# Perceiver kernel on one core: the first head pair's key rows by selection matmuls, early keys and values among the maxima

## The reference

```
q = einsum(layernorm(x), wq) * 8 ** -0.5          # 16 heads of 8
k = einsum(ctx, wk);  v = einsum(ctx, wv)         # 2048 keys per batch
logits = einsum(k, q) + mask                      # the mask is all zeros in these inputs
x = x + einsum(softmax(logits), v) @ wo
```

## Time and profile before

| | |
|---|---|
| runs | 303.33 us median of 3 (302.24 to 303.79) |
| profiled execution | span 302.6 us from first to last instruction; no other time is given for it |
| instructions | 10,326 |
| PE, DVE, ACT, POOL busy | 94%, 75%, 69%, 23% of the span |
| DMA | 28.06 MB, 93 GB/s on average |

### The profile page before, as it was taken

One profiled execution on the slowest core, in us unless ns is written; L12 is line 12 of the kernel. 1 busy time (PEld: TensorE's weight loads), 2 busy tenths in 40 slices (PEclk: granted clock), 3 DMA queues, 4 the chain that ended last, 5 costly groups with the idle time before them and its releaser, 6 DMA issues.

```text
span 302.6 us, 10326 instructions
## 1 busy us (share of the span) xinstructions
PE 284.7 (94%) x4336; PEld 186.6 (62%) x4340; DVE 226.9 (75%) x376; ACT 207.3 (69%) x447; POOL 71.0 (23%) x140
## 2 busy tenths in 40 slices
PE   7965999999999999899999899999999999999995
PEld 6553666666767675453656567676766665436675
DVE  5864789999999985464478998988999970744583
ACT  4638489889898888723445898989989987233350
POOL 6595500020011102431021865000011020110001
PEclk9995899999999999999999999999999999999999
DMA  7984513632222280233200036422221200000000
GB/s 238 410 248 138 169 41 106 232 119 71 87 70 80 80 301 6 104 122 105 89 3 0 3 84 213 136 79 74 79 82 54 57 2 2 0 3 2 0 0 20
DMA packets 10898, 28.06 MB, mean 93 GB/s; under 512 B 2241, under 2 KB 3329, under 8 KB 10466
## 3 DMA queue, kind: packets, MB, share of 16 engines
q1 hardware_dynamic: 10776, 27.16, 27.3%
q10 hardware_dynamic: 74, 0.20, 0.2%
HBM read 20.74 MB, written 6.62 MB: 90 GB/s over the span
## 4 chain that ended last, share of the span: by engine, by line
PE 75%; DVE 14%; DMA 3%; ACT 3%; POOL 2%; issue 2%; ACTq 1%; DVEq 0%; POOLq 0%
PE bank L1082 73%; DVE mx L835 7%; DMA k_first_rows<-kparts 2%; ACT probs L557 1%; DMA kpair<-k_first_rows 1%; DVE kparts L804 1%; DVE k_rest L801 1%; DVE s_neg L894 1%; DVE st L745 1%; POOL m_rows L438 1%; PE bank L1387 1%; ACTq L276 1%; PE bank L1427 0%; DVE xn L764 0%; DVE negm L842 0%
## 5 line engine op out<-in xcount | busy, mean ns | idle before, releaser
L835 DVE TENSOR_REDUCE mx<-bank 128x2 f32<-128x1024 f32 x128 | 153.0, 1222 | 19.1 <-PE bank L1082 15.2
L557 ACT ACTIVATE probs<-bank 128x512 f32<-128x512 f32 x256 | 139.3, 595 | 20.7 <-PE bank L1082 16.7
L1082 PE MATMUL bank<-q_exp,kpair 64*128 64x128 bf16 x1024 | 84.8, 218 | 1.9 <-ACT probs L557 1.2
L1082 PE MATMUL bank<-probs,v_all 128*9 128x128 f32 x2048 | 80.1, 274 | 1.1 <-ACT probs L557 1.0
L1082 PE MATMUL bank<-kpair,q_rows 64*128 64x512 bf16 x256 | 73.9, 388 | 5.8 <-DMA kpair<-k_first_rows 5.8
L1082 PEld LDWEIGHTS bank<-q_exp,kpair 64*128 64x128 bf16 x1024 | 55.3, 94 | 31.5 <-ACT probs L557 13.2
L1082 PEld LDWEIGHTS bank<-probs,v_all 128*9 128x9 f32 x2048 | 43.2, 90 | 17.0 <-ACT probs L557 4.0
L438 POOL CAST m_rows<-negm 128x2 bf16<-128x2 f32 x32 | 7.1, 222 | 136.5 <-DVE negm L842 136.5
L1082 PEld LDWEIGHTS bank<-kpair,q_rows 64*128 64x128 bf16 x256 | 22.6, 93 | 7.9 <-issue 6.4
L494 ACT ACTIVATE v_all<-bank 128x512 f32<-128x512 f32 (+1 forms) x20 | 10.5, 538 | 11.9 <-PE bank L1082 11.9
L629 ACT ACTIVATE s_sb<-bank 128x512 f32<-128x512 f32 x16 | 8.3, 602 | 11.9 <-PE bank L1082 11.9
(11 more groups left out here) (226 smaller groups left out, 348.2 us busy)
## 6 DMA issues: line engine op xcount, KB each, us to landing
k_scratch<-kparts SPq DMA_DIRECT2D x24, 256.0 KB, 2.8
kpair<-k_scratch SPq DMA_DIRECT2D x62, 96.0 KB
kpair<-k_scratch SPq DMA_DIRECT2D x62, 64.0 KB
ctxT_s<-in_ctxT SPq DMA_DIRECT2D x4, 512.0 KB, 5.8
mask_s<-in_mask SPq DMA_DIRECT2D x2, 1024.0 KB, 10.3
kpair<-k_scratch SPq DMA_DIRECT2D x62, 32.0 KB
wM<-in_packM SPq DMA_DIRECT2D x1, 1728.0 KB, 7.0
wB<-in_packB SPq DMA_DIRECT2D x1, 599.0 KB, 4.9
```

Source lines behind the costliest of these rows:

```text
L557: act.activation(probs[:, j % 4, :], bank[:, 4 + j % 2, :], ACT.Exp).then_inc(S("exp_done"), 1)
L835: V.tensor_reduce(mx[n % 2][:, w, :], bank[:, 2 * (w % 2):2 * (w % 2) + 2, :], AX.X, ALU.max) \
L1082: return T.matmul(out_, lhsT=lhsT, rhs=rhs, start=start, stop=stop, **kw)
```

## The change

First, the logarithms of the gumbel step move from the start of ACT's cross(0) to the start of ACT's program. Second, SP issues the two masks ahead of batch 1's context. Third, the first pair's key rows no longer go through HBM: for each of the four key tiles PE multiplies a new 0/1 table selk with the three parts (first_k, three matmuls), and ACT copies the result from PSUM into kpair, adding ones to the spare rows (first_rows). Two of DVE's four middle-part casts go to ACT (mid_k). Fourth, the second mask is tested half on ACT and half on DVE. Fifth, early_k and stage_k of layer 0 move into cross(0), where they are interleaved with the first maxima and with the values of batch 1, which already stood there. The banks of the early keys and values change accordingly. POOL's program changes in one place only: one memset of kpair fewer.

```diff
-EARLY_BANK = ((2, 3, 6, 7), (2, 3, 2, 7))
-V_BANK = ((2, 3, 6, 2, 4, 5, 7, 4), (7, 3, 7, 6, 4, 5, 4, 5))
+EARLY_BANK = ((6, 7, 6, 7), (2, 3, 2, 7))
+V_BANK = ((2, 3, 6, 7, 4, 5, 4, 5), (7, 3, 7, 6, 4, 5, 4, 5))
...
@@ SP @@
+            for b in range(B):
+                sp.dma_start(mask_s[:, b, :], mask[b, 0, :, :]).then_inc(S(f"in_mask{b}"), 16)
             for c in range(2, 4):
                 sp.dma_start(ctxT_s[:, c * 1024:(c + 1) * 1024], ctxT[:, c * 1024:(c + 1) * 1024]) \
                     .then_inc(S(f"in_ctx{c}"), 16)
-            for b in range(B):
-                sp.dma_start(mask_s[:, b, :], mask[b, 0, :, :]).then_inc(S(f"in_mask{b}"), 16)
...
             store_k(0, 0, 0)
-            sp.wait_ge(S("k_low"), 4)
-            sp.dma_start(kfirst, kparts[0:2 * HD, :, 0:SK]).then_inc(S("k_first"), 16)
             store_k(0, 0, 1)
-            sp.wait_ge(S("k_first"), 16)
-            sp.wait_ge(S("k_ones"), U)
-            first_head(sp, 0)
+            sp.wait_ge(S("k_ones"), U - 1)
             cross_k(0, 1)
...
@@ POOL @@
-            for i in range(U):
+            for i in range(1, U):
                 pool.memset(kpair[i][:, :].bitcast(F32), two_ones).then_inc(S("k_ones"), 1)
...
@@ ACT, in cross @@
                 if l == 0:
-                    act.wait_ge(S("gum_sum"), 1)
-                    act.activation(gum[:, 33:34], gum[:, 32:33], ACT.Ln).then_inc(S("gum_lse"), 1)
-                    act.wait_ge(S("gum_lse"), 1)
-                    act.activation(gum[:, 62:63], gum[:, 33:34], ACT.Exp, scale=-1.0)
+                    for i in range(4):
+                        stage_k(0, i)
+                        prep_v(0, 4 + i)
...
@@ ACT, at the start @@
+            act.wait_ge(S("gum_sum"), 1)
+            act.activation(gum[:, 33:34], gum[:, 32:33], ACT.Ln).then_inc(S("gum_lse"), 1)
+            act.wait_ge(S("gum_lse"), 1)
+            act.activation(gum[:, 62:63], gum[:, 33:34], ACT.Exp, scale=-1.0)
             for c in range(3):
                 prep_k(0, c)
             norm("n0")
             prep_k(0, 3)
             query(0)
-            for i in range(4):
-                stage_k(0, i)
+            def mid_k(c):
+                act.wait_ge(S("k_rest1"), c + 1)
+                copy(kparts[:, 1, c * 512:(c + 1) * 512], k_rest[c][:, :]).then_inc(S("k_mid"), 1)
+            def first_rows(c):
+                act.wait_ge(S("k_sel"), c + 1)
+                act.activation(kpair[0][:, c * 512:(c + 1) * 512], bank[:, k_bank(0, c), :], ACT.Identity,
+                               bias=A_("kone", 1)).then_inc(S("k_first"), 1)
+            mid_k(2)
+            mid_k(3)
+            act.wait_ge(S("in_A2"), 16)
+            first_rows(0)
             prep_v(0, 0)
+            first_rows(1)
+            prep_v(0, 1)
+            first_rows(2)
+            first_rows(3)
             act.wait_ge(S("in_mask1"), 16)
-            act.activation(probs[:, :, :].rearrange("p w n -> p (w n)"), mask_s[:, 1, :], ACT.Abs,
+            act.activation(probs[:, 0:2, :].rearrange("p w n -> p (w n)"), mask_s[:, 1, SK // 2:SK], ACT.Abs,
                            accum_out=flag_f[:, 1:2]).then_inc(S("mask1_sum"), 1)
-            act.wait_ge(S("k_ones"), U)
-            act.wait_ge(S("k_first"), 16)
-            first_head(act, 1)
             for k in range(2):
                 put_rows(0, k)
-            for c in range(1, V_EARLY[0]):
-                prep_v(0, c)
+            prep_v(0, 2)
+            prep_v(0, 3)
             cross(0)
...
@@ DVE @@
+            dve.wait_ge(S("in_mask1"), 16)
+            V.tensor_scalar(probs[:, 2:4, :].rearrange("p w n -> p (w n)"), mask_s[:, 1, 0:SK // 2], 0.0, None,
+                            ALU.not_equal, ALU.add, accum_out=flag_f[:, 3:4])
             dve.wait_ge(S("mask1_sum"), 1)
...
@@ PE @@
+            def first_k(c):
+                pe.wait_ge(S("k_low"), c + 1)
+                for s in range(PARTS):
+                    last = mm(bank[:, k_bank(0, c), :], selk[:, s * P:(s + 1) * P],
+                              kparts[0:4 * HD, s, c * 512:(c + 1) * 512], start=(s == 0), stop=(s == PARTS - 1))
+                last.then_inc(S("k_sel"), 1)
...
@@ PE, in cross, in the loop over the first six a_head pairs @@
+                    if l == 0 and i == 0:
+                        pe.wait_ge(S("v_copied"), 4)
+                        early_k(0, 0)
+                    elif l == 0 and i == 1:
+                        pe.wait_ge(S("q_rows2"), 2)
+                        prep_v(0, 4)
+                    elif l == 0 and i == 2:
+                        early_k(0, 1)
+                    elif l == 0 and i == 3:
+                        prep_v(0, 5)
+                        early_k(0, 2)
+                    elif l == 0 and i == 4:
+                        prep_v(0, 6)
+                        early_k(0, 3)
+                    elif l == 0 and i == 5:
+                        prep_v(0, 7)
...
@@ PE, ahead of the branch @@
             query()
-            for i in range(4):
-                early_k(0, i)
-            for c in range(2):
-                pe.wait_ge(S("k_staged"), c + 1)
-                prep_v(0, c)
+            pe.wait_ge(S("in_selk"), 16)
+            first_k(0)
+            prep_v(0, 0)
+            first_k(1)
+            prep_v(0, 1)
+            first_k(2)
+            first_k(3)
             pe.wait_ge(S("q_split"), 1)
-            pe.wait_ge(S("k_rest1"), 4)
...
             place_q()
-            pe.wait_ge(S("k_staged"), 4)
+            pe.wait_ge(S("k_first"), 4)
             prep_v(0, 2)
+            prep_v(0, 3)
             pe.wait_ge(S("flag_rows"), 1)
-            mm(bank[0:1, 7, 0:1], flag_f[:, 0:1], ones_col, stop=False)
-            mm(bank[0:1, 7, 0:1], flag_f[:, 2:3], ones_col, start=False).then_inc(S("flag_sum"), 1)
+            pe.wait_ge(S("v_copied"), 1)
+            mm(bank[0:1, 2, 0:1], flag_f[:, 0:1], ones_col, stop=False)
+            mm(bank[0:1, 2, 0:1], flag_f[:, 3:4], ones_col, start=False, stop=False)
+            mm(bank[0:1, 2, 0:1], flag_f[:, 2:3], ones_col, start=False).then_inc(S("flag_sum"), 1)
```

More of the change, by code:

```diff
@@ L53 @@
 ROUTED_SCALE = 2.5
-PK_A = dict(x=0, wk0=256, ident=384, wq0=512, wv0=640, wo0=768)
+PK_A = dict(x=0, wk0=256, ident=384, wq0=512, wv0=640, wo0=768, kone=896)
 PK_A1_W = 512
-PK_A_W = 896
+PK_A_W = 897
 PK_B = dict(w_oT=0, w_uv=128, w_uk=192, wk1=256, wv1=384, wq1=512, wo1=640, aq=768, ak=896, av=1024,
@@ L78, with perceiver_kernel @@
 X_UNIT = (9, 10, 12, 13, 14, 15)
-def perceiver_kernel(nc, packA, packB, packC, packR, packM, ffnW, ffnb, mask, ctxT, selq_d, rep_d, cm_d, out):
+def perceiver_kernel(nc, packA, packB, packC, packR, packM, ffnW, ffnb, mask, ctxT, selq_d, selk_d, rep_d, cm_d, out):
     with ExitStack() as ctx:
@@ L268, in load_head @@
                 eng.dma_start(kpair[u][row:row + times * HD, :], src).then_inc(S(f"k_loaded{u}"), 16)
[L270 to L276, removed]
         block = ctx.enter_context(nc.Block())
@@ L587, in cross @@
                 if l == 0:
-                    act.wait_ge(S("gum_sum"), 1)
-                    act.activation(gum[:, 33:34], gum[:, 32:33], ACT.Ln).then_inc(S("gum_lse"), 1)
-                    act.wait_ge(S("gum_lse"), 1)
-                    act.activation(gum[:, 62:63], gum[:, 33:34], ACT.Exp, scale=-1.0)
[L592 to L597, removed]
+                    for i in range(4):
+                        stage_k(0, i)
+                        prep_v(0, 4 + i)
+                else:
+                    act.wait_ge(S("q_proj"), 3)
+                    copy(q_parts[:, 0, P:2 * P], x_out, SCALE).then_inc(S("q_full"), 1)
+                    copy(q_rest[:, P:2 * P], x_out, SCALE).then_inc(S("q_full"), 1)
+                    for c in range(4, 8):
+                        prep_v(l, c)
                 put_qe(0)
@@ L802, in prep_k @@
                     .then_inc(S("k_rest1"), 1)
-                dve.wait_ge(S("k_rest1"), k + 1)
-                V.tensor_copy(kparts[:, 1, cols], k_rest[c][:, :]).then_inc(S("k_mid"), 1)
+                if l or c < 2:
+                    dve.wait_ge(S("k_rest1"), k + 1)
+                    V.tensor_copy(kparts[:, 1, cols], k_rest[c][:, :]).then_inc(S("k_mid"), 1)
             def query(l):
@@ L978, in _ @@
             dve.wait_ge(S("flag_sum"), 1)
-            V.tensor_copy(flag_i[:, :], bank[0:1, 7, 0:1]).then_inc(S("flag"), 1)
+            V.tensor_copy(flag_i[:, :], bank[0:1, 2, 0:1]).then_inc(S("flag"), 1)
             for k in range(2, 4):
@@ L1256, in a_ready @@
                 def a_ready(n, w):
-                    if w == 0:
-                        pe.wait_ge(S(f"k_loaded{n % U}"), K_LOADS * 16 * ((g0 + n) // U + 1))
+                    if g0 + n == 0:
+                        pe.wait_ge(S("k_first"), w + 1)
+                    elif w == 0:
+                        pe.wait_ge(S(f"k_loaded{n % U}"), K_LOADS * 16 * ((g0 + n) // U + (n % U > 0)))
                     if 4 * (g0 + n) + w >= 2:
@@ L1325, in cross @@
```

(18 more changed lines are left out.)

19 lines of the change are left out of this document (8 added, 11 removed).

## The result

The change makes the kernel slower. Four runs of the changed kernel have a median of 312.23 us (311.73 to 312.82), beside them the kernel before 302.93 us (302.24 to 303.79); the ratio is 1.0279, with a 95% interval of 1.0253 to 1.0305. The forecast was 310.3 us, in a range of 305.5 to 312.5.

A forecast was written before the change was run, and what follows sets the result against it. PE was taken to bound the loop, with POOL's splits delaying put_exp(0). +5.5 for POOL and +1.5 for the clock made +7.0: span 309.6, median 310.3 us, range 305.5 to 312.5.

The forecast's parts named there:

- The frame: PE paces the loop at an unchanged 5.34 us a step; the change can move only put_exp(0), base 34.78.
- the main case: Before the loop, POOL's splits wait for early keys behind the branch, with a second clock fall: 310.3 us, chance 0.55.
- Logarithms, masks, selection: Before the first scores: logarithms and masks gain nothing; fourth selection ends near 16.4, q's placing at 17.2.
- Flag and branch: Ahead of the first scores: flag written near 19.9, branch 3.63, scores at 25.1; removed round trip worth 0.85 us.
- The rival in which the branch is short in its new place: At the mask test, the branch's fetch overlaps the flag wait: scores at 21.5, 305 us (304 to 306.6), chance 0.12.
- The clock: PE's idle before the loop may drop its clock again: 1.5 us taken, from no loss to 2.6.
- The base: Span 302.6, 0.7 below the three-run median 303.33, same shift put on the median; put_exp(0) at 34.78.
- No second fall: PE's clock does not fall again before the loop, POOL alone costs +5.5: 308.8 us, chance 0.22.
- PE's list as the end: Before the loop, POOL finds time for its splits and PE's list ends at 38: +3.2, 306.5 us, chance 0.05.
- A fetch of the branch's far side ahead of the flag: At the branch, PE's fetch runs ahead of the flag: put_exp(0) at 33.3, -1.5, 301.8 us, chance 0.06.

The follow-up runs named there:

- e1_splits_late: Changed kernel with K_LATE = (4, 4): POOL does all four splits of batch 1's keys behind the maximum rows; 305.78 us, ratio 1.0072.
- e9_keys_ahead: Changed kernel with all four early key projections ahead of the branch again, POOL's order as in the change, no fill; 302.65 us, ratio 1.0001.
- e5_before_logs_masks: Kernel before with only the logarithms at the start of ACT's program and the masks ahead of batch 1's context; 307.77 us, ratio 1.0124.
- e3_no_branch: Changed kernel without the flag's load and the branch, the masked copy left out; 306.45 us, ratio 1.0104.
- e2_warm_loop: Changed kernel with 14 matmuls without a use in PE's wait ahead of put_exp(0); 308.69 us, ratio 1.0166.
- e4_before_no_branch: Kernel before without the flag's load and the branch, the masked copy left out; 303.50 us, ratio 0.9991.
- e7_early_two: Changed kernel with two early projections and 14 fill matmuls ahead of the branch, two splits ahead of the first maximum rows; 302.13 us, ratio 0.9945.
- e8_early_four: Changed kernel with all four early projections and 6 fill matmuls ahead of the branch, two splits ahead of the maximum rows; 301.87 us, ratio 0.9935.
- e6_late_warm_branch: Changed kernel with all splits behind the maximum rows and 22 matmuls without a use ahead of the flag wait; 305.18 us, ratio 1.0040.

## Why the prediction was right, and where its sum was off

**The frame held.** Everything acts at put_exp(0), the loop's step is unchanged, and POOL's three splits set the moment: the first three things named as signs of the main case (POOL idle until about 28 for ACT's copy, no idle before m_rows, a branch over 3 us) stand in the profile after, and so do PE's wait before m_rows and the slow first steps. e1_splits_late and e9_keys_ahead show that it takes two things in company: the keys behind the branch, and POOL's order left as it was.

**Logarithms, masks, selection: right.** ACT's first key copy is at 7.86 (7.84 before; 0.4 late was allowed). q's placing ends at 16.78 (17.2 forecast), ACT's four copies of key rows at 16.86 (17.0). e9_keys_ahead bears out that together with the shorter way of the first rows they come to about nothing. What the prediction did not say is that the masks' place depended on the fifth part; e5_before_logs_masks showed that.

**Flag and branch: right, but forecast 1.1 too late.** The flag was forecast at 19.9 and written at 19.21, since DVE could start its share of the masks at 15.01, not 15.5; the load of the flag took 0.49, not 0.73; the branch took 3.61, where 3.63 was taken. First scores at 24.04, not 25.1; the terms as written, 19.95 + 1.1 + 3.63 + 0.3, make 25.0. The ends 0.1 and 4.7 given for the branch were wide of need. The rival in which the branch is short in its new place fell with it: it took 3.41 to 3.97 us in all nine traces that have one. The Trainium skill's "Advanced Engine Details and Errata", section "Control Flow Timing", has about 108 ns for a compare and branch; no trace here agrees with it. What PE waits for in the branch can be narrowed by the queue of instructions (packets, MB, share), in after and in e3_no_branch:

```profile
q8 instruction: 37, 0.61, 0.8%
...
q8 instruction: 34, 0.56, 0.8%
```

All nine kernels with the branch have 37 packets, the two without it 34, and in each of the nine exactly one packet moves while the branch runs. The Trainium skill's "Runtime: NRT & Kernel Launch", section "Instruction fetch mechanics", by which a taken branch out of the fetched window stalls for the fetch of its target, fits this; it gives no time for the stall, and no run here shows that the fetch fills all of the 3.4 to 4.0 us.

**put_exp(0): 4.7 later, 5.5 forecast** (5.4 by the forecast's own 40.2 less 34.78). Of the 1.1 that the scores came early, 0.6 arrived at POOL (first split at 27.41, not 28.0), because the first projection took 2.07, all of it at the low clock, and not 1.6. The splits took 11.5 (11.6). The forecast's order of events was right; the flag was the term that was a little too large.

**The clock: the term that was too small.** Taken at 1.5, bounded by 2.6, measured at 3.2. The step that failed was the bound: it carried over "the 5.9 us it stayed low after work resumed" from the start of the kernel. In the loop the clock stayed at 1.2 GHz for some 9.6 us, from 39.5 to about 49.1 (0.71 on average from 48 to 50), and in e3_no_branch for some 9.3. Why it stayed low for longer is open; that the 3.2 are its price is shown by e2_warm_loop.

**The base: 1.4.** The same shift was put on the median as on the span, the span being "0.7 below the median of the three runs". A span has to be compared with its own execution's time, 1.95 above it in the median of the runs, and by that measure this one was slower than all three. The trace of e4_before_no_branch, the old kernel without the branch and with no change in time, has put_exp(0) at 33.72, 1.06 sooner than the base of 34.78: 0.57 of that at the first scores, the rest because the clock came back sooner (0.73 granted from 28 to 32, 0.52 in before). The expectations of e1_splits_late and e3_no_branch, summed from the same base, both came out 1.3 low. A base from one execution is uncertain by its runs' spread, 302.24 to 303.79 here, and the prediction did not carry that.

So the terms are 4.7 + 3.2 + 1.4 = 9.3 where 5.5 + 1.5 = 7.0 was forecast: one too large, one too small, one not seen. (The 7.0 was put on 303.33, and a fourth run makes the median of before 302.93; hence 312.23 is only 1.9 above the forecast of 310.3.) That 312.23 lies within the range, 0.3 below its top, is in part luck. The top was built from 6.2 for POOL and 2.6 for the clock; the clock went past its bound and the base was in neither, while POOL stayed 1.5 below its own.

**The other rivals.** No second fall (308.8): the fall came; e2_warm_loop, which keeps it away, took 308.69. PE's list as the end (306.5): PE's list was ready at 36.3 and waited 3.17; e1_splits_late, which makes that case, took 305.78. A fetch of the branch's far side ahead of the flag: nothing of it in any trace, the branch takes over 3.4 us in all nine.

## What to carry to other kernels

Before removing a wait, look for what else lies under it: here a 3.6 us branch stood beside the DMA round trip. Taking the branch away alone gave nothing, and taking the round trip away brought the first scores 1.9 us sooner, not the 5.8 of idle that the trace put down to it. When work is moved behind a late event, follow each consumer's own order: an engine that is 77% idle (POOL) became the bound because three jobs that had slack stood ahead of one that had none, and reversing that order alone gave 6.5 us back. Work that fills a forced wait can also hold PE's clock up, as the early projections and the fill do under the branch in e7_early_two and e8_early_four.

## What was not expected of the hardware

The branch did not stop matmuls that stood ahead of it in PE's program. The branch of e7_early_two, and its PE in order of time:

```profile
L1568 PEldq COMPARE_BRANCH  x1: 3406/3406/3406, 20.4 to 20.4; - x1
...
19.14 1.98 PE L1096 MATMUL bank<-ctxT_s,wA 128*128 128x512 f32 x4
20.96 3.19 PE L1096 MATMUL bank<-selq,ident_b 128*128 128x512 bf16 x14
24.08 0.39 PE L1096 MATMUL bank<-kpair,q_rows 64*128 64x512 bf16 x2
```

With two projections and 14 fill matmuls ahead of it, PE worked from 18.92 to 24.15 while the branch ran from 20.4 for 3.41, and the scores followed without idle. Where the fill stands matters: 14 matmuls behind the wait for the flag left the flag's load 0.25 after the flag, 22 ahead of that wait (e6_late_warm_branch) put it 0.8 behind.

The clock did not come back as soon as PE was busy again. From 39.5 to 48 PE is busy for 4.18 of 4.50 and 4.00 of 4.00 us, with 0.50 granted throughout, while after the first fall it came back early in 28 to 32 (0.92 on average), some 5 us after the scores began. The falls themselves came after waits of 3.17 in this kernel and 3.33 in e3_no_branch; in the profiled run of e9_keys_ahead there was none after 2.12.
